# Attention stage: x given transposed and split on GpSimd, projections dealt out three halves to a graph

## The chip, the cores and the metric

The kernel runs on one core of a Trainium2 chip. A time is device microseconds (us) of one execution. TensorE (PE) does matmuls and transposes into PSUM; VectorE (DVE), ScalarE (ACT) and GpSimd (POOL) do the rest; SyncE (SP) issues most DMAs. Each engine works through its own instructions in order and waits on semaphores.

## What is computed

64 graphs of 128 nodes with 256 features, and a 128x128 adjacency for each. First an attention layer with eight heads, and a layernorm; the change touches only this. Then three layers of graph attention, each with a feed-forward part, and a last layernorm.

```
q = heads(x @ Wq); k = heads(x @ Wk); v = heads(x @ Wv)        # 8 heads of 32
scores = where(adj, q k^T / sqrt(32), -inf)                    # 128 x 128 per head
out = softmax(scores) @ v
x = layernorm(x + relu(out) @ Wo)
... three layers: scores = leaky(si + sj + b), softmax, agg, layernorm, gelu ffn, layernorm
```

## The kernel before

All work on attention is in the first `with ExitStack()` block, in steps t = 0 to 15 of four graphs each (j = 0 to 3; i = 4t + j). A step's tokens are 512 columns. The products with weights are made to higher precision from pairs: a number is split into a rounded part (`hi`) and a rest (`lo`), and `split_product` (its matmul is L45) sums three products for each half k of the 256 features. So a projection of 512 columns is two parts of three matmuls each, called halves in the text.

The order on each engine is written out by hand, and the engines are pipelined against each other over steps:

- TensorE, in step t and graph j: transposes of the softmax numerators of heads 4 to 7 (L383) and 0 to 3 (L389), of the reciprocal sums (L395), the products with v (L401, "PV"), the scores of graph i+2 (L365), the output product with Wo (L45 on `attT`). Between them `fill` puts work for coming steps: in graphs 0 to 2 two of the six projections of step t+1 (four q/k, two v), in graph 3 the eight transposes (`transpose_x`, L337) of x of step t+2 from `xq` into the PSUM banks `A`.
- ScalarE casts these banks to `xT_hi` (L439), copies the projections to SBUF (`proj_copy`, L444), takes the exponentials (L449), and copies transposes (L461, L469).
- VectorE subtracts for `xT_lo` (L511), adds the mask to the scores and takes maxima (`masked_scores`, L523: a graph's eight heads), and between or behind these the residual `y` (L573); it normalizes (L560), splits (L563, L565), and takes layernorm statistics (L535, L539).
- In graph 2 of step t, `masked_scores` is that of graph 0 of step t+1, and it needs the mask of step t+1, the first of the two that GpSimd makes.
- GpSimd (`body`, L313): `make_masks(t+1)` (L298 is the mask of this stage, L299 to L306 make another for the later stages), then `ln_group(t)`, the layernorm of step t, which waits for VectorE's statistics `mv_out`. These are made in graph 0 of step t+1. `hold_pool` waits and then runs a tiny instruction (`fence_pool`, L147).
- SyncE (`body`, L256), step t: load `xq` of t+2, store the second mask, wait for the last `y` of step t, load x and adjacency of t+2, wait for the layernorm of t, store it to `hist` (L270).

`mask1`, `hist` and `mask_hist` serve the later stages. `steps` runs t = 0 to 13 in a loop of two, and 14 and 15 behind it.

Of the kernel before, what the change touches and what calls it, by code (L numbers as in the profile page):

```python
# [24 lines left out]
F32 = mybir.dt.float32  # L25
# [5 lines left out]
P = 128  # L31
# [18 lines left out]
def gnn_kernel(nc, x_in, adj, Wq, Wk, Wv, Wo, attn_w, attn_b, W1, b1, W2, b2, g1, beta1, g2, beta2, out):  # L50
# [28 lines left out]
    with ExitStack() as whole:  # L79
# [91 lines left out]
        with ExitStack() as ctx:  # L171
# [4 lines left out]
            xq = sb("xq", [P, GROUP, D])  # L176
# [6 lines left out]
            xT = [sb("xT_hi", [P, KT, TOK], F32R), sb("xT_lo", [P, KT, TOK], F32R)]  # L183
# [17 lines left out]
            wa_split, xq_ld = sems("wa_split", "xq_ld")  # L201
            x_ld = sems("x_ld_even", "x_ld_odd")
            (masks_made, xT_made, xT_hi_out, xT_lo_out, proj_made, proj_out, s_made, scored, peaked, exped,
             pT_made, pT_out_b, pT_out_a, pv_made, den_inv, rden_out, rdenT_made, rdenT_out, att_out,
             attT_hi_out, attT_lo_out, wo_made, y_out, bn_out, eye_made, eye_added) = sems(
                "masks_made", "xT_made", "xT_hi_out", "xT_lo_out", "proj_made", "proj_out", "s_made", "scored",
# [32 lines left out]
            def _(e):  # L239
# [3 lines left out]

                for sem in stored + mask1_st:
                    e.sem_inc(sem, START)
                e.dma_start(xq[:], block_of(x_g, 0)).then_inc(xq_ld, 16)
# [4 lines left out]
                e.wait_ge(xT_made, 2)  # L251
                e.dma_start(xq[:], block_of(x_g, 1)).then_inc(xq_ld, 16)
# [31 lines left out]
            def _(e):  # L284
# [22 lines left out]

                make_masks(0, 0, 0)

# [17 lines left out]
            def _(e):  # L327
                e.wait_ge(ident_set, 1)

                def transpose_x(t1, k):  # L330

                    if k == 0:
                        e.wait_ge(xq_ld, 16 * (t1 + 1))
                    if not isinstance(t1, int) or t1:
                        e.wait_ge(proj_out, 6 * t1 - 1 + k)
                    for j in range(GROUP):
                        mm = e.transpose(A[k][:, j * N:(j + 1) * N], xq[:, j, k * P:(k + 1) * P], ident[:])  # L337
                    mm.then_inc(xT_made, 1)

                def project(t1, par, n, parts=(0, 1)):  # L340

                    bank = A[n % 2]
                    if n == 0 and 0 in parts:
                        e.wait_ge(xT_hi_out, 2 * (t1 + 1))
                        e.wait_ge(xT_lo_out, 2 * (t1 + 1))
                    if n >= 2 and 0 in parts:
                        e.wait_ge(proj_out, 6 * t1 + n - 1)
                    if n < 4:
                        mm = split_product(e, bank, (w_hi, w_lo), xT,
                                           lambda w, k: w[:, n % 2, k, (n // 2) * P:(n // 2 + 1) * P],  # L350
                                           lambda x, k: x[:, k, :], parts)
                    else:
                        for h in parts:
                            j = 2 * (n - 4) + h
                            mm = split_product(e, bank[:, h * D:(h + 1) * D], xT, (w_hi, w_lo),
# [13 lines left out]
                def fill(t, par, j, half, a1, a2, parts=(0, 1)):  # L369

                    if j < 3 and a1:
                        project(t + 1, 1 - par, 2 * j + half, parts)
                    if j == 3 and half == 0 and a2:
                        for k in parts:
                            transpose_x(t + 2, k)

                def body(q, par, a1, a2):
                    t = 2 * q + par
                    for j, i, _, (has2, t2, par2, j2) in graphs(q, par, a1):
# [5 lines left out]
                        fill(t, par, j, 0, a1, a2, parts=(0,))  # L385
# [5 lines left out]
                        fill(t, par, j, 0, a1, a2, parts=(1,))  # L391
# [17 lines left out]
                        fill(t, par, j, 1, a1, a2)  # L409
# [5 lines left out]
                for k in range(KT):  # L415
                    transpose_x(0, k)
# [4 lines left out]
                for k in range(KT):  # L421
                    transpose_x(1, k)
# [5 lines left out]
            def _(e):  # L428
# [7 lines left out]

                def xT_hi(t1, k):
# [759 lines left out]
```

## Time and profile before

| | us |
|---|---|
| median of 3 runs (1758.45 to 1760.78) | 1760.39 |
| the profiled execution | 1757.66 |
| its span | 1755.9 |
| TensorE busy in the span | 1631.8 (93%) |
| VectorE | 1372.9 (78%) |
| ScalarE | 1246.0 (71%) |
| GpSimd | 1232.0 (70%) |

The shares are means over the attention stage (to about 430 us) and the later stages. A share tells how much an engine works, not when it is free. So stretches of the attention stage and the order in which things stand on each engine are read beside it. In a timeline, what stands in brackets is how long the engine had been idle before, and which instruction of which engine ended it.

### The profile page before, as it was taken

What the parts mean: (1) busy time and instruction counts of PE and PEld (TensorE: products, weight loads), DVE (VectorE), ACT (ScalarE), POOL (GpSimd) and SP (SyncE); (2) the same over time, 40 slices, a digit from 0 to 9 for tenths busy, and PEclk for the clock granted to TensorE, in tenths of its full rate; (3) what the DMA queues carried; (4) which work ended last, traced back from release to release, by engine and by line L of the source; (5) the groups of instructions that cost most, each with busy time, mean ns of one, the idle gap of its engine ahead of it and who ended that gap; (6) DMA issues with size and microseconds to landing.
All of it is one profiled execution on the core that took longest, in us unless ns stands there. A gap on an engine that the chain in (4) does not pass through costs nothing.

```text
span 1755.9 us, 40514 instructions
## 1 busy us (share of the span) xinstructions
PE 1631.8 (93%) x12032; PEld 1441.2 (82%) x12032; DVE 1372.9 (78%) x5392; ACT 1246.0 (71%) x2884; POOL 1232.0 (70%) x2087
## 2 busy tenths in 40 slices
PE   4999999996599999999989999999999999999994
PEld 3877777774499899899979899899888888888894
DVE  2888888887678878787777877788787888888862
ACT  2888888885477767767757777767766777777763
POOL 3354445543368777777868778777868999999996
PEclk8999999998699999999999999999999999999997
DMA  6132223322212212212213122212211222222211
GB/s 195 50 96 83 78 78 96 96 77 74 81 40 96 96 36 72 72 37 70 72 36 96 61 70 72 72 36 72 72 36 61 70 74 72 73 94 72 73 49 48
DMA packets 152118, 127.41 MB, mean 73 GB/s; under 512 B 16512, under 2 KB 145024, under 8 KB 152064
## 3 DMA queue, kind: packets, MB, share of 16 engines
q1 hardware_dynamic: 145024, 124.30, 22.5%
q10 hardware_dynamic: 7040, 2.51, 0.6%
q8 instruction: 19, 0.31, 0.1%
q14 instruction: 35, 0.29, 0.1%
HBM read 89.04 MB, written 37.75 MB: 72 GB/s over the span
## 4 chain that ended last, share of the span: by engine, by line
PE 51%; POOL 16%; DVE 5%; issue 2%; ACT 1%; POOLq 0%; DVEq 0%; ACTq 0%
PE ps L45 22%; PE ps L879 22%; PE ps L852 3%; POOL xo L792 2%; POOL gnn_n L160 2%; POOL gnn_norm L786 2%; PE ps L866 2%; POOL gnn_norm L160 2%; POOL gnn_fin L805 2%; POOL inv L155 2%; DVE gnn_junk L1004 2%; PE ps L844 1%; POOL gnn_hb L775 1%; POOL gnn_hb L771 1%; PE ps L859 1%
## 5 line engine op out<-in xcount | busy, mean ns | idle before, releaser
L879 PE MATMUL ps<-gnn_w_hi,gnn_g_hi 128*128 128x256 f32 x1536 | 434.1, 283 | 0.0
L879 PE MATMUL ps<-gnn_w_lo,gnn_g_hi 128*128 128x256 f32 x1536 | 429.0, 279 | 0.0
L879 PE MATMUL ps<-gnn_w_hi,gnn_g_lo 128*128 128x256 f32 x1536 | 428.7, 279 | 0.0
L974 ACT ACTIVATE gnn_g_hi<-ps,b_cols 128x512 fp32r<-128x512 f32 x384 | 264.6, 689 | 206.9 <-PE ps L45 206.9
L45 PE MATMUL ps<-gnn_hT_hi,gnn_w_hi 128*128 128x512 f32 x768 | 339.5, 442 | 4.2 <-DVE gnn_g_lo L1075 4.2
L1075 DVE TENSOR_TENSOR gnn_g_lo<-ps,gnn_g_hi 128x512 fp32r<-128x512 f32 x384 | 262.7, 684 | 95.9 <-ACT ps L975 95.5
L45 PE MATMUL ps<-gnn_hT_hi,gnn_w_lo 128*128 128x512 f32 x768 | 304.0, 396 | 0.0
L45 PE MATMUL ps<-gnn_hT_lo,gnn_w_hi 128*128 128x512 f32 x768 | 303.8, 396 | 0.0
L879 PEld LDWEIGHTS ps<-gnn_w_lo,gnn_g_hi 128*128 128x128 f32 x1536 | 288.9, 188 | 2.2
L879 PEld LDWEIGHTS ps<-gnn_w_hi,gnn_g_hi 128*128 128x128 f32 x1536 | 288.8, 188 | 2.2
L879 PEld LDWEIGHTS ps<-gnn_w_hi,gnn_g_lo 128*128 128x128 f32 x1536 | 288.7, 188 | 0.0
L975 ACT ACTIVATE ps<-ps,b_cols 128x512 f32<-128x512 f32 x384 | 250.6, 653 | 0.0
L1004 DVE CUSTOM_DVE_ANT_0 gnn_junk<-x,aw 128x256 f32<-128x256 f32 x384 | 222.7, 633 | 0.5 <-PEq L171 0.5
L449 ACT ACTIVATE att_probs<-att_probs,att_neg_peak 128x128 f32<-128x128 f32 x512 | 199.1, 393 | 10.7 <-DVE att_neg_peak L530 10.7
L45 PEld LDWEIGHTS ps<-gnn_hT_hi,gnn_w_lo 128*128 128x128 f32 x768 | 144.8, 189 | 34.5
L45 PEld LDWEIGHTS ps<-gnn_hT_hi,gnn_w_hi 128*128 128x128 f32 x768 | 145.5, 189 | 32.9 <-DVE gnn_g_lo L1075 5.0
L45 PEld LDWEIGHTS ps<-gnn_hT_lo,gnn_w_hi 128*128 128x128 f32 x768 | 145.5, 190 | 28.0
L775 POOL TENSOR_TENSOR gnn_hb<-gnn_hb,affine 128x256 f32<-128x256 f32 x192 | 156.3, 846 | 7.2 <-POOL gnn_hb L771 6.0
L949 ACT ACTIVATE gnn_hT_hi<-ps,beta_cols,g_cols 128x512 fp32r<-128x512 f32 x96 | 74.9, 780 | 109.8 <-PE ps L866 109.8
L152 POOL TENSOR_TENSOR inv<-gnn_mv,eps 128x4 f32<-128x4 f32 x96 | 19.5, 203 | 186.8 <-DVE gnn_mv L1143 153.6
L1067 DVE TENSOR_TENSOR gnn_res<-ps,gnn_hb 128x256 f32<-128x256 f32 x192 | 79.9, 416 | 85.3 <-PE ps L879 84.7
L771 POOL TENSOR_TENSOR gnn_hb<-gnn_n,affine 128x256 f32<-128x256 f32 x192 | 138.9, 755 | 8.5 <-POOL gnn_n L160 7.2
(126 smaller groups left out, 3952.2 us busy)
## 6 DMA issues: line engine op xcount, KB each, us to landing
hist<-xo SPq DMA_DIRECT2D x48, 512.0 KB, 3.7
x<-hist SPq DMA_DIRECT2D x48, 512.0 KB, 3.8
aw<-in_L_gnn_attn_w SPq DMA_DIRECT2D x48, 256.0 KB, 4.1
gmask<-mask_hist SPq DMA_DIRECT2D x48, 256.0 KB, 4.0
att_xq<-in_x SPq DMA_DIRECT2D x16, 512.0 KB, 4.6
att_xl<-in_x SPq DMA_DIRECT2D x16, 512.0 KB, 3.7
gnn_fin<-hist SPq DMA_DIRECT2D x16, 512.0 KB, 3.9
out<-gnn_fin SPq DMA_DIRECT2D x16, 512.0 KB, 3.0
```

Source lines behind the costliest of these rows:

```text
L45: last = pe.matmul(out, w_of(w[a], k), x_of(x[b], k), start=(n == 0 and k == 0), stop=(n == len(terms) - 1 and k == 1))
L160: last = e.tensor_scalar(dest[:, j, :], y[:, j, 0:D], inv[:, 2, j:j + 1], inv[:, 3, j:j + 1], ALU.mult, ALU.add)
L449: ins = e.activation(probs[b][:, h, :], probs[b][:, h, :], ACT.Exp, bias=neg_peak[b][:, h:h + 1], scale=SCALE, accum_out=den[b][:, h:h + 1])
L771: ins = e.tensor_tensor(hb[par1][:, j, :], n1[:, j, :], row(l, 0), ALU.mult)
L775: ins = e.tensor_tensor(hb[par1][:, j, :], hb[par1][:, j, :], row(l, 2), ALU.add)
L879: mm = e.matmul(FF2[j % 2], g[a][:, m, j * N:(j + 1) * N], V[b][:, m, :], start=(n == 0), stop=(n == len(terms) - 1))
L949: e.activation(hT[0][:, k, :], HT[k], ACT.Identity, bias=shift, scale=gain)
L974: e.activation(g[0][:, m, :], FF1[FFB[m]], ACT.Gelu, bias=bias)
L975: e.activation(FF1[FFB[m]], FF1[FFB[m]], ACT.Gelu, bias=bias).then_inc(gelu_out, 1)
L1004: ins = e.tensor_tensor_reduce(out=junk[:, j, n, :], in0=x[par2][:, j, 0:D], in1=aw[par2][:, n, :], scale=1.0, scalar=0.0, op0=ALU.mult, o ...
L1067: e.tensor_tensor(y2[:, j, :], FF2[j % 2], hb[par][:, j, :], ALU.add).then_inc(y2_out, 1)
L1075: e.tensor_tensor(g[1][:, m, :], FF1[FFB[m]], g[0][:, m, :].bitcast(F32), ALU.subtract).then_inc(g_lo_out, 1)
```

## The change

The host gives x also as `xT`: per step 128 rows (features) of 1024 numbers (two halves of the features, 512 tokens each), 4 KB a row. SyncE loads it into `xT_raw` in place of `xq`. GpSimd makes `hi` and `lo` from it with `split_xT`, four casts and four subtractions of 128x256, at the start of its step t for step t+2. `xT` becomes two pairs of buffers, used by even and odd steps. TensorE's transposes, ScalarE's casts and VectorE's subtractions for it go. `fill` hands out the twelve halves as three to each of four graphs, beginning in graph 3 of the step before. ScalarE's `proj_copy` calls are spread in the same way. In `masked_scores` the residual stands after four heads in each graph, before that only in graph 3.

```diff
@@ sync @@
+                def load_xT(t):
+                    e.dma_start(xT_raw[:].rearrange("p k n -> p (k n)"),
+                                xT_in[bass.ds(t, 1)].rearrange("o p n -> p (o n)")).then_inc(xT_ld, 16)
...
-                e.wait_ge(xT_made, 2)
-                e.dma_start(xq[:], block_of(x_g, 1)).then_inc(xq_ld, 16)
+                e.wait_ge(xT_lo_out, 1)
+                load_xT(1)
...
                 def body(q, par, more):
                     t = 2 * q + par
                     if more:
-                        e.wait_ge(xT_made, 2 * (t + 2))
-                        e.dma_start(xq[:], block_of(x_g, t + 2)).then_inc(xq_ld, 16)
+                        e.wait_ge(xT_lo_out, t + 2)
+                        load_xT(t + 2)
@@ gpsimd @@
+                PARTS = [(k, slice(n * TOK // 2, (n + 1) * TOK // 2)) for k in range(KT) for n in range(2)]
+
+                def split_xT(t1, par):
+
+                    hold_pool(e, xT_ld, 16 * (t1 + 1))
+                    if not isinstance(t1, int) or t1 >= 2:
+                        hold_pool(e, proj_made, 6 * (t1 - 1))
+                    hi, lo = xT[par]
+                    for k, half in PARTS:
+                        ins = e.tensor_copy(hi[:, k, half], xT_raw[:, k, half])
+                    ins.then_inc(xT_hi_out, 1)
+                    e.wait_ge(xT_hi_out, t1 + 1)
+                    for k, half in PARTS:
+                        ins = e.tensor_tensor(lo[:, k, half], xT_raw[:, k, half], hi[:, k, half].bitcast(F32), ALU.subtract)
+                    ins.then_inc(xT_lo_out, 1)
+
+                split_xT(0, 0)
                 make_masks(0, 0, 0)
+                split_xT(1, 1)
...
                 def body(q, par, a1, a2):
                     t = 2 * q + par
+                    if a2:
+                        split_xT(t + 2, par)
                     if a1:
                         e.wait_ge(masks_made, 2 * (t + 1))
                         e.wait_ge(peaked, GROUP * t + 1)
@@ tensor @@
                     if n == 0 and 0 in parts:
-                        e.wait_ge(xT_hi_out, 2 * (t1 + 1))
-                        e.wait_ge(xT_lo_out, 2 * (t1 + 1))
-                    if n >= 2 and 0 in parts:
+                        e.wait_ge(xT_lo_out, t1 + 1)
+                    if 0 in parts and (n >= 2 or not isinstance(t1, int) or t1):
                         e.wait_ge(proj_out, 6 * t1 + n - 1)
...
-                def fill(t, par, j, half, a1, a2, parts=(0, 1)):
-
+                def fill(t, par, j, slot, a1, a2):
+
+                    n, part = divmod(3 * ((j + 1) % GROUP) + slot, 2)
                     if j < 3 and a1:
-                        project(t + 1, 1 - par, 2 * j + half, parts)
-                    if j == 3 and half == 0 and a2:
-                        for k in parts:
-                            transpose_x(t + 2, k)
+                        project(t + 1, 1 - par, n, (part,))
+                    if j == 3 and a2:
+                        project(t + 2, par, n, (part,))
@@ scalar @@
-                        if j > 0 and a1:
-                            proj_copy(t + 1, 1 - par, 2 * (j - 1))
-                            proj_copy(t + 1, 1 - par, 2 * (j - 1) + 1)
+                        if a1:
+                            proj_copy(t + 1, 1 - par, (0, 2, 3, 5)[j])
...
+                        if a1 and j in (0, 2):
+                            proj_copy(t + 1, 1 - par, 1 if j == 0 else 4)
...
-
-                for k in range(KT):
-                    xT_hi(0, k)
@@ vector @@
-                            masked_scores(i + 2, t2, par2, j2, residual, at=4 if j == GROUP - 1 else NH)
+                            masked_scores(i + 2, t2, par2, j2, residual, at=4)
```

GpSimd, from the end of one layernorm (`xo`) to the masks of the next step; `xT_ld` counts the landed loads of the transposed x.

```order
 L160 TENSOR_SCALAR xo<-y,inv 128x256 x4
 L168 REGISTER_ALU
-L316 REGISTER_ALU [waits ln_out]
-L317 ISA [waits masks_made]
+L145 ISA [waits ln_out]
+L147 TENSOR_TENSOR fence_pool<-half_neg 128x1 [waits xT_ld]
+L145 REGISTER_ALU
+L147 TENSOR_TENSOR fence_pool<-half_neg 128x1 [waits proj_made]
+L321 CAST att_xT_hi<-att_xT_raw 128x256 x4
+L325 TENSOR_TENSOR att_xT_lo<-att_xT_raw,att_xT_hi 128x256 [waits xT_hi_out]
+L325 TENSOR_TENSOR att_xT_lo<-att_xT_raw,att_xT_hi 128x256 x3
```

Between the layernorm and the masks there now stand a wait for the load and eight operations.

SyncE at the turn from one step to the next, of the changed kernel.

```order
L274 ISA [waits ln_out]
L274 DMA hist<-xo 128x4x256
L263 REGISTER_ALU
L245 ISA [waits xT_lo_out]
L245 DMA att_xT_raw<-in_xT 128x1024
L266 REGISTER_ALU
L267 ISA [waits masks_made]
L267 DMA mask_hist<-att_mask_1 128x4x128
```

The load has the place that the load of `xq` had, behind the store of the layernorm; what it waits for is GpSimd's split, no longer TensorE's transposes.

TensorE in graph 3, before:

```order
L383 MATMUL ps<-ident,att_probs 128x128 x3
L333 ISA
L335 ISA [waits xq_ld]
L337 MATMUL ps<-ident,att_xq 128x128 [waits proj_out]
L337 MATMUL ps<-ident,att_xq 128x128 x3
L386 REGISTER_ALU
L389 MATMUL ps<-ident,att_probs 128x128 [waits y_out,exped]
```

and now:

```order
L397 MATMUL ps<-ident,att_probs 128x128 x3
L359 REGISTER_ALU
L361 ISA [waits xT_lo_out]
L45 MATMUL ps<-att_xT_hi,att_w_hi 128x512 [waits proj_out]
L45 MATMUL ps<-att_xT_lo,att_w_hi 128x512
L45 MATMUL ps<-att_xT_hi,att_w_lo 128x512
L400 REGISTER_ALU
L403 MATMUL ps<-ident,att_probs 128x128 [waits y_out,exped]
```

Where four transposes waited for a load, the first half of the next-but-one step's projections waits for GpSimd's subtractions.

## Rows read from the trace of the kernel before

**Rows 1.** Windows of a stretch: start:end us, length, busy (instructions) per engine, clock, DMA, GB/s
```profile
202.00:229.00 27.00, 25.22 (x282) 20.74 (x284) 23.36 (x114) 22.72 (x93) 14.74 (x24) 1.00 0.28 78
```

**Rows 2.** Timeline of SyncE's DMA issues: start us, us, engine line operation out<-in
```profile
73.86 0.40 SPq L270 DMA_DIRECT2D hist<-xo  x1
74.52 0.38 SPq L260 DMA_DIRECT2D att_xq<-in_x  x1
...
196.55 0.40 SPq L270 DMA_DIRECT2D hist<-xo  x1
197.50 0.38 SPq L260 DMA_DIRECT2D att_xq<-in_x  x1
...
392.54 0.40 SPq L270 DMA_DIRECT2D hist<-xo  x1
```

**Rows 3.** Timeline of GpSimd over one step, the same columns
```profile
192.25 0.20 POOL L152 TENSOR_TENSOR inv<-mv,eps 128x4 f32<-128x4 f32 x1 [12.47 <-DVE mv L539]
...
194.19 2.19 POOL L160 TENSOR_SCALAR xo<-y,inv 128x256 f32<-128x256 f32 x4
...
197.31 2.10 POOL L298 TENSOR_SCALAR att_mask<-att_adjl 128x512 f32<-128x512 int32 x1
...
202.94 0.34 POOL L147 TENSOR_TENSOR fence_pool<-half_neg 128x1 f32<-128x1 f32 x2
```

**Rows 4.** Timeline of VectorE over the same step
```profile
191.82 0.28 DVE L539 BATCH_NORM_AGGREGATE mv<-att_a_stats 128x2 f32<-128x6 f32 x3
...
205.81 0.29 DVE L523 CUSTOM_DVE_ANT_0 att_probs<-ps,att_mask 128x128 f32<-128x128 f32 x1
...
209.33 1.28 DVE L511 TENSOR_TENSOR att_xT_lo<-ps,att_xT_hi 128x512 fp32r<-128x512 f32 x2
210.53 0.41 DVE L560 SCALAR_TENSOR_TENSOR att_att<-ps,att_rdenT 128x256 f32<-128x256 f32 x1
...
215.88 0.28 DVE L539 BATCH_NORM_AGGREGATE mv<-att_a_stats 128x2 f32<-128x6 f32 x3
```

**Rows 5.** Timeline of TensorE, two places in this stage and one of a later stage
```profile
195.50 0.39 PE L45 MATMUL ps<-att_xT_lo,att_w_hi 128*128 128x512 f32 x1
195.73 0.40 PE L45 MATMUL ps<-att_xT_hi,att_w_lo 128*128 128x512 f32 x1
...
209.47 0.65 PE L401 MATMUL ps<-att_probsT,att_v 128*32 128x128 f32 x16
...
893.72 0.73 PE L45 MATMUL ps<-gnn_hT_hi,gnn_w_hi 128*128 128x512 f32 x1 [3.51 <-DVE gnn_g_lo L1075]
```

**Rows 6.** Part 6 of the page: DMA issues, count, KB each, us to landing
```profile
att_xq<-in_x SPq DMA_DIRECT2D x16, 512.0 KB, 4.6
att_xl<-in_x SPq DMA_DIRECT2D x16, 512.0 KB, 3.7
...
out<-gnn_fin SPq DMA_DIRECT2D x16, 512.0 KB, 3.0
```

**Rows 7.** Groups of GpSimd's instructions by line and shape: count | busy us, mean ns
```profile
L775 POOL TENSOR_TENSOR gnn_hb<-gnn_hb,affine 128x256 f32<-128x256 f32 x192 | 156.3, 846 | 7.2 <-POOL gnn_hb L771 6.0
...
L786 POOL TENSOR_TENSOR gnn_norm<-gnn_norm,affine 128x256 f32<-128x256 f32 x192 | 135.7, 740 | 8.1 <-POOL gnn_norm L160 6.8
...
L160 POOL TENSOR_SCALAR xo<-y,inv 128x256 f32<-128x256 f32 x64 | 35.2, 563 | 0.0
...
L306 POOL TENSOR_SCALAR att_mask<-att_eye_sum 128x512 f32<-128x512 f32 x16 | 31.1, 1943 | 1.1
...
L285 POOL MEMSET ident<- 128x128 f32 x1 | 0.2, 205 | 0.3 <-POOLq L1184 0.3
```

**Rows 8.** Windows of a later stretch, columns as in rows 1
```profile
890.00:895.00 5.00, 1.49 (x4) 1.10 (x4) 4.32 (x8) 1.43 (x3) 3.12 (x4) 0.88 0.00 2
```

**Rows 9.** Timeline of ScalarE at the start
```profile
27.03 1.07 ACT L444 COPY att_qk<-ps 128x512 f32<-128x512 f32 x2 [19.12 <-issue]
```

More of the change, by code:

```diff
@@ L182, in gnn_kernel @@
             mask1 = [sb(f"mask1_{i}", [P, GROUP, N]) for i in range(2)]
-            xT = [sb("xT_hi", [P, KT, TOK], F32R), sb("xT_lo", [P, KT, TOK], F32R)]
+            xT = [[sb(f"xT_hi{i}", [P, KT, TOK], F32R), sb(f"xT_lo{i}", [P, KT, TOK], F32R)] for i in range(2)]
             qk = [sb(f"qk{i}", [P, 4, TOK]) for i in range(2)]
@@ L384, in body @@
                         mm.then_inc(pT_made, 1)
-                        fill(t, par, j, 0, a1, a2, parts=(0,))
+                        fill(t, par, j, 0, a1, a2)
                         e.wait_ge(exped, 2 * i + 2)
@@ L390, in body @@
                         mm.then_inc(pT_made, 1)
-                        fill(t, par, j, 0, a1, a2, parts=(1,))
+                        fill(t, par, j, 1, a1, a2)
                         e.wait_ge(pT_out_b, i + 1)
@@ L408, in body @@
                             scores(i + 2, par2, j2)
-                        fill(t, par, j, 1, a1, a2)
+                        fill(t, par, j, 2, a1, a2)
                         e.wait_ge(attT_hi_out, i + 1)
@@ L420, in _ @@
                 scores(0, 0, 0)
-                for k in range(KT):
-                    transpose_x(1, k)
+                for slot in range(3):
+                    fill(-1, 1, 3, slot, True, True)
                 e.wait_ge(scored, 1)
@@ L455, in body @@
                     for j, i, has1, _ in graphs(q, par, a1):
-                        if j > 0 and a1:
-                            proj_copy(t + 1, 1 - par, 2 * (j - 1))
-                            proj_copy(t + 1, 1 - par, 2 * (j - 1) + 1)
+                        if a1:
+                            proj_copy(t + 1, 1 - par, (0, 2, 3, 5)[j])
                         e.wait_ge(pT_made, 2 * i + 1)
                         e.copy(probsT[:, 4:8, :].rearrange("p h n -> p (h n)"), PB[1]).then_inc(pT_out_b, 1)
-                        if j == 3 and a2:
-                            for k in range(KT):
-                                xT_hi(t + 2, k)
                         if has1 and j < 3:
@@ L488, in _ @@
                     proj_copy(0, 0, n)
-                for k in range(KT):
-                    xT_hi(1, k)
                 e.wait_ge(peaked, 1)
@@ L506, in split_weights @@
                     e.tensor_tensor(w_lo[:, pair], w_raw[:, pair], w_hi[:, pair].bitcast(F32), ALU.subtract).then_inc(wa_split, 1)
-                def xT_lo(t1):
-                    for k in range(KT):
-                        e.wait_ge(xT_hi_out, 2 * t1 + k + 1)
-                        e.tensor_tensor(xT[1][:, k, :], A[k], xT[0][:, k, :].bitcast(F32), ALU.subtract).then_inc(xT_lo_out, 1)
                 def masked_scores(i, t_, par, j, between=None, at=NH):
@@ L1188 @@
     arrays, args = {}, []
+    x = np.asarray(inputs["x"])
+    B, N, D = x.shape
+    laid = dict(inputs)
+    laid["xT"] = (x.reshape(B // GROUP, GROUP, N, D // P, P).transpose(0, 4, 3, 1, 2)
+                  .reshape(B // GROUP, P, D // P * GROUP * N))
+    names.insert(1, "xT")
     for name in names:
-        a = np.ascontiguousarray(inputs[name])
+        a = np.ascontiguousarray(laid[name])
         arrays[f"in_{name}"] = a
```

34 lines of the change are left out of this document (9 added, 25 removed).

## The prediction

> **What bounds the kernel now.** I read the span by stages first. The change touches the attention stage alone, sixteen steps of four graphs that fill the span to about 430 us; the rest stays as it is. In the stage's middle the stretches show TensorE busy 25.2 of 27 us, VectorE 23.4, ScalarE 22.7, and GpSimd 14.7 [rows 1]: two engines are nearly full, a third close behind, and GpSimd looks half idle. That share invites the change, and it is the number not to trust, since it says nothing of when GpSimd is free. So next I read SyncE's DMA issues and the order on GpSimd. SyncE stores step 0's result at 73.86 and step 13's at 392.54 [rows 2]: 318.68 us for 13 steps, 24.51 us a step. On GpSimd [rows 3] one step is: the layernorm of the step before (from 192.25, last piece ends at 194.19 + 2.19 = 196.38), then the masks of the step after, the first of which VectorE needs (197.31 to 199.41), then three more operations and a long wait. On VectorE [rows 4] the statistics that release the layernorm end at 191.82 + 0.28 = 192.10 (call this point V), and the first use of the new mask comes at 205.81 (call it M); the next V is at 215.88 + 0.28 = 216.16. So today the mask is ready 6.4 us before its use, and GpSimd sets nothing.
>
> **The change, part by part.** *What it takes away.* Per step, 8 transposes on TensorE, 2 casts on ScalarE and 2 subtractions on VectorE; the VectorE pair takes 1.28 us in the fourth graph [rows 4]. The fill of TensorE is evened out: now 4 halves in each of three graphs, then 3 in each of four. A half is three matmuls that start 0.23 us apart [rows 5], 0.70 us. In the first three graphs TensorE is what limits: 24.51 / 4 = 6.13 us a graph, less 0.70, is 5.43, and VectorE loses its 1.28 us in the fourth. If nothing else came late, a step would take about 22 us (4 x 5.43 = 21.7, and something for waits). Doing the residual after four heads instead of eight costs nothing; it only shortens the wait of the next transposes.
>
> *What it adds, and where.* GpSimd's step now begins with the split of x for step t+2, ahead of the masks of t+1. Its input is loaded by SyncE, in order, directly behind the store of the layernorm that GpSimd has just finished. So the load cannot start while GpSimd is busy elsewhere: it starts when GpSimd becomes free for it. In the kernel before the load stood at the same place, but its user was TensorE in the fourth graph, ten us later; now its user is the very next instruction on GpSimd. Behind that waiting instruction are queued the split, the masks of t+1, and the next layernorm. Who waits for them: TensorE (first half of step t+2's projections, in the fourth graph) and, later and harder, VectorE (the mask, at the end of the third graph).
>
> From V to M, each term:
> - layernorm: 192.10 to 196.38, 4.28 us [rows 3, 4].
> - store issued 0.17 after it, the load behind it 0.95 later, in other steps 0.66 [rows 2]: 0.81. Together 0.98.
> - landing. The load that it replaces, of equal size and with the same neighbours, takes 4.6 us; another load of 512 KB takes 3.7, the quickest transfer of 512 KB 3.0 [rows 6]. The new one is one run of 4 KB per partition. I take 4.2, between the first two, and keep 3.0 to 4.7.
> - two fences on GpSimd, 0.34 and a gap: 0.40 [rows 3].
> - four casts of 128x256. No cast stands on GpSimd here. The nearest row, a two-step scalar operation of the same size, takes 0.563; half of the 128x512 comparison is 0.97; a memset of 128x128 takes 0.205, so that 0.31 for 256 columns is a floor [rows 7]. I take the nearest: 2.25, and keep 1.2 to 3.9.
> - a wait between, 0.10, and four subtractions of 128x256 with two inputs: 0.740 to 0.846 [rows 7], taken 0.80: 3.20.
> - from there to the first mask 0.50 (today 0.93 with the layernorm's own wait in it), the mask 2.0, VectorE's start 0.1 [rows 3].
>
> Sum: 4.28 + 0.98 + 4.20 + 0.40 + 2.25 + 0.10 + 3.20 + 0.50 + 2.0 + 0.1 = 18.0 us.
>
> The row of the two-step operation gives 2.2 ns per column. The Trainium skill, GPSIMD Engine Reference, section 4.1 Engine selection, says instead that with one input GpSimd runs at roughly line rate, which would make a cast about 0.3 us by my estimate from that page; the sum would fall by 1.0 us, 13 us over the stage, and the sign would stay. No run so far shows which.
>
> From M to the next V the order of work is VectorE's, and today's rows give it: 216.16 - 205.81 = 10.35 us [rows 4]. The two subtractions go from it (1.28 us from 209.33), but the product that they stood before has to wait for TensorE anyway: the PV matmuls run from 209.47 to 210.12, so it moves from 210.53 to 210.2 at best [rows 4, 5]. That leaves 10.0. The cycle V, M, V closes on itself, once a step: 18.0 + 10.0 = 28.0 us. At the free pace VectorE would be ready for the mask 22 - 10.0 = 12 us after V and so stands about 6 us; by then everything else is late by the same.
>
> *The clock.* In the loop TensorE will have gaps of about 2 us (until the split is done) and 3 us (until the mask is). After a gap of 3.51 us in a later stage [rows 5] the granted clock of the stretch falls to 0.88 of full, that is to 1.2 GHz of 2.4 for part of it [rows 8]. At half speed PV and the transposes after M could come some 0.5 us later. I put in 0.3, range 0 to 1: 28.3 us a step.
>
> Steps 1 to 13 each have a split in front of the next mask: 13 x (28.3 - 24.51) = +49 us. Step 14 splits nothing and runs at the free pace, -2; step 0 has its mask long before and runs at the free pace, -2; step 15 has the earlier residual, -1. At the start ScalarE issues its small loads only after the two casts, from about 7.9, and does its first copy at 27.03 after 19.12 us of issuing [rows 9]; without the casts it may begin up to 6 us earlier, and TensorE's projections wait for it. The DMA engines are full then, so I take 4, range -1 to 6, and 1 for the second split that leaves VectorE. The first split on GpSimd ends at about 11, as late as VectorE's today. Together -10.
>
> **Sum** against the profiled execution: 1757.7 + 49 - 10 = 1797. That execution lies 2.7 below the median of 1760.4, so the median becomes **1799 us**, 2.2% slower.
>
> **The rivals.**
> *A. Faster: GpSimd is hidden.* Then all fifteen steps with a successor run at the free 22 us: 15 x -2.5 = -38, and -5 at the start: 1717. For it: GpSimd's share, and that it idles after the masks. Against it: that idle time is after its late work, not before. It decides if V to M is under 12 us, so that load, casts and subtractions together are under 3.6, less than the shortest landing and two casts.
> *B. No change.* The +49 must shrink to the 10 us of gains: a step of 25.3 us, V to M 15.3, load and split together 6.9 instead of 9.6. The floors of the three add up to 3.0 + 1.2 + 3.0 = 7.2. Time 1757 to 1764. This rival is the lower bound of all unknown terms at once.
> *C. Slower still.* Landing 4.7, casts at 0.97 (3.9) and subtractions at 0.85 (3.4) make V to M 20.4, and with 0.7 us of clock a step 31.1 us: 13 x 6.6 - 10 = +76, 1836. For it: the split runs beside VectorE's copies in SBUF, and the comparison row is slow without a reason that I can see.
> *D. The change doesn't do what it says.* If SyncE's load were ahead of the store, the landing would hide and it would be A. The order of its queue excludes that: it waits for the layernorm, stores, and only then loads.
> The Trainium skill, DMA: Bandwidth & Descriptors, gives a fixed 2.0 us and 436 GB/s for a transfer; by that the load lands in 3.2 us (my estimate from that page), the step is 1.0 us shorter and the median 1786; still the forecast's side.
>
> **How the numbers follow.** Forecast (a step of 26.3 to 30, V to M of 16 to 20) 0.74; C 0.16; B 0.05; A 0.05. The range begins with landing and casts both four fifths of the way to their floors (3.2 and 1.4, a step of 26.4 with 0.2 of clock: 13 x 1.9 - 10 = +15, 1775) and ends with C: 1773 to 1836. What a measurement of this kernel can tell from no change is about 0.2%, 3.5 us. Chances: faster by more 0.06, within 0.03, slower by more 0.91.
>
> **What would show it.** In the changed kernel: steps of about 28 us between SyncE's stores; GpSimd idle about 5 us after each layernorm, released by the DMA of the transposed x; VectorE idle 5 to 6 us before the first head of the third graph's scores, released by GpSimd's mask; TensorE idle about as long in the fourth graph, first on GpSimd's split, then on VectorE's residual. The first doubt is the casts' duration, the second the landing. The prediction is wrong in kind if VectorE does not wait for the mask, or if steps of 22 us appear before step 14.

## The result, and the profile after

| | before | after |
|---|---|---|
| median of 4 runs, us | 1760.57 | 1811.70 (1808.87 to 1812.87) |
| span of the profiled execution | 1755.9 | 1810.1 |
| us a step, stores of step 0 to 13 | 24.51 | 28.40 |
| TensorE busy in the span | 1631.8 (93%) | 1649.3 (91%) |

The changed kernel is slower, by a ratio of 1.0291 (95% interval 1.0273 to 1.0309). 1799 had been predicted, with 1773 to 1836 as the range. SyncE's DMA issues answer to [rows 2]; the columns here, and in the timelines below, are start us, us, engine, line, operation, out<-in, and in brackets the idle time before and what ended it:

```profile
74.53 0.40 SPq L274 DMA_DIRECT2D hist<-xo  x1
...
215.82 0.40 SPq L274 DMA_DIRECT2D hist<-xo  x1
216.75 0.35 SPq L245 DMA_DIRECT2D att_xT_raw<-in_xT  x1
...
443.68 0.40 SPq L274 DMA_DIRECT2D hist<-xo  x1
...
468.00 0.39 SPq L274 DMA_DIRECT2D hist<-xo  x1
```

(443.68 - 74.53) / 13 = 28.40 us. So 369.15 - 318.68 = 50.5 us of the span's +54.2 lie in steps 1 to 13. The rest is small: the first store comes 0.7 later than in before, step 14 takes 24.32 (in before its store is at 416.52, a step of 23.98), and what follows it takes 1342.1, before 1339.4.

One step on GpSimd after, to be laid beside [rows 3]:

```profile
213.49 2.17 POOL L160 TENSOR_SCALAR xo<-y,inv 128x256 f32<-128x256 f32 x4
221.28 0.34 POOL L147 TENSOR_TENSOR fence_pool<-half_neg 128x1 f32<-128x1 f32 x2 [5.62 <-DMA att_xT_raw<-in_xT]
221.56 1.49 POOL L321 CAST att_xT_hi<-att_xT_raw 128x256 fp32r<-128x256 f32 x4
223.13 3.02 POOL L325 TENSOR_TENSOR att_xT_lo<-att_xT_raw,att_xT_hi 128x256 fp32r<-128x256 f32 x4
...
226.38 1.95 POOL L302 TENSOR_SCALAR att_mask<-att_adjl 128x512 f32<-128x512 int32 x1
```

The layernorm ends at 215.66, SyncE stores at 215.82 and loads at 216.75, and GpSimd stands idle until the load has landed. Only then come the casts, the subtractions and, at 226.38, the mask that began 0.93 us behind the layernorm in before.

The same step on VectorE, beside [rows 4]:

```profile
211.12 0.28 DVE L535 BATCH_NORM_AGGREGATE mv<-att_a_stats 128x2 f32<-128x6 f32 x3
...
224.00 0.70 DVE L557 CAST att_attT_hi<-att_att 128x256 fp32r<-128x256 f32 x1
224.73 0.83 DVE L559 TENSOR_TENSOR att_attT_lo<-att_att,att_attT_hi 128x256 fp32r<-128x256 f32 x1
228.48 0.06 DVE L142 MEMSET fence_dve<- 128x1 f32 x1 [2.91 <-POOL att_mask L302]
228.52 0.29 DVE L519 CUSTOM_DVE_ANT_0 att_probs<-ps,att_mask 128x128 f32<-128x128 f32 x1
...
237.73 0.42 DVE L567 TENSOR_TENSOR y<-ps,att_xl 128x256 f32<-128x256 f32 x1 [1.86 <-PE ps L45]
...
240.96 0.28 DVE L535 BATCH_NORM_AGGREGATE mv<-att_a_stats 128x2 f32<-128x6 f32 x3
```

V is at 211.40, M at 228.52, the next V at 241.24: 17.1 and 12.7 us. In the step behind it M comes at 258.12 and V at 269.19: 16.9 and 11.1. VectorE is idle 2.91 us in front of the mask.

The waits of the stretch 80 to 440 us; the columns are who waits, for whom, us in total, times, longest:

```profile
POOL inv L152 <- DVE mv L535: 77.5, 13, 7.5
POOL fence_pool L147 <- DMA att_xT_raw<-in_xT: 71.0, 13, 5.6
...
DVE fence_dve L142 <- POOL att_mask L302: 32.9, 12, 2.9
...
PE ps L403 <- DVE y L567: 25.0, 13, 2.2
```

The chain is in these lines: GpSimd waits for the load, VectorE for GpSimd, TensorE for VectorE's residual, once in every step. In its windows (columns as in [rows 1]):

```profile
202.00:229.00 27.00, 23.12 (x240) 17.43 (x238) 19.70 (x103) 18.94 (x78) 15.22 (x29) 1.00 0.27 78
229.00:256.00 27.00, 23.71 (x227) 18.59 (x228) 20.55 (x106) 18.41 (x77) 13.81 (x29) 0.87 0.25 78
```

VectorE is busy 19.7 us of 27 instead of 23.4, and ScalarE 18.9 instead of 22.7: no engine is full any longer. In the second window the granted clock is 0.87 of full, so for a part of it TensorE has 1.2 GHz instead of 2.4, and the step took 29.9 us. Three of the thirteen steps are like that (step lengths of 29.90, 29.85 and 29.86 between stores), the other ten take 27.95 on average. Two of these ten have the lower clock too, for a smaller part of the step:

```profile
273.61:302.15 28.54, 24.47 (x242) 18.78 (x240) 20.40 (x108) 18.65 (x78) 16.32 (x29) 0.94 0.26 73
330.14:358.05 27.91, 24.58 (x242) 18.44 (x240) 20.41 (x110) 19.00 (x80) 16.35 (x29) 0.94 0.25 75
```

The eight steps at full clock take 27.89 on average.

### The profile page after: what moved, and what is told of

It is laid out like the page before. It is cut to its first block, busy times and chain, and to the rows that moved or that the text cites. A ratio compares the mean times of both kernels' runs of the same rounds, so it can differ in the third digit from the quotient of the medians.

```text
span 1810.1 us, 40318 instructions
## 1 busy us (share of the span) xinstructions
PE 1649.3 (91%) x11904; PEld 1433.1 (79%) x11904; DVE 1357.8 (75%) x5360; ACT 1224.4 (68%) x2852; POOL 1303.6 (72%) x2245
## 4 chain that ended last, share of the span: by engine, by line
PE 49%; POOL 16%; DVE 5%; issue 2%; ACT 1%; POOLq 0%; DVEq 0%; ACTq 0%
PE ps L45 21%; PE ps L871 21%; PE ps L844 3%; POOL xo L784 2%; POOL gnn_n L160 2%; POOL gnn_norm L778 2%; PE ps L858 2%; POOL gnn_norm L160 2%; POOL gnn_fin L797 2%; DVE gnn_junk L996 2%; POOL inv L155 2%; PE ps L836 1%; POOL gnn_hb L767 1%; POOL gnn_hb L763 1%; PE ps L851 1%
## 5 line engine op out<-in xcount | busy, mean ns | idle before, releaser
L457 ACT ACTIVATE att_probs<-att_probs,att_neg_peak 128x128 f32<-128x128 f32 x512 | 199.2, 392 | 25.5 <-DVE att_neg_peak L526 25.3
```

The lines of the kernel that those rows point to most:

```text
L457: ins = e.activation(probs[b][:, h, :], probs[b][:, h, :], ACT.Exp, bias=neg_peak[b][:, h:h + 1], scale=SCALE, accum_out=den[b][:, h:h + 1])
```

## The experiments

Each is compared with the kernel before, run on the same chip; its median was 1755.5 to 1757.8 there, against 1760.6 beside the changed kernel. So kernels measured on different chips are compared by their ratios, and steps by their traces. My theory was the cycle V, M, V with the load in it. The rivals were that the order on GpSimd alone (split ahead of mask) does it, that the early residual or the dealing of the halves does, or that the clock does.

### Masks first, whole

```diff
-                    if a2:
-                        split_xT(t + 2, par)
                     if a1:
                         e.wait_ge(masks_made, 2 * (t + 1))
                         e.wait_ge(peaked, GROUP * t + 1)
                         make_masks(q + (par + 1) // 2, 1 - par, t + 1)
+                    if a2:
+                        split_xT(t + 2, par)
```

> The changed kernel with GpSimd's step in another order: both masks of step t+1 first, then the split of step t+2. Theory T (the mask comes late because the load of the transposed x and the split stand in front of it): VectorE's waits for the mask go. But the split then ends about 17.9 us after VectorE's statistics, and TensorE wants it at about 15.5 (the first half in the fourth graph), so a wait of 2 to 3 us moves to TensorE: a step of about 27 us for 28.4, 1793 us, 1785 to 1800. Rival R (not GpSimd but TensorE's new distribution sets the pace, three halves in the fourth graph in front of the next statistics): no change, 1811.

Measured: 1795.28 us, 1.0223 (ratio to the kernel before; 1.0205 to 1.0241), 27.36 us a step, as expected. One wait of 80 to 440 us, and the end of GpSimd's step:

```profile
PE ps L45 <- POOL att_xT_lo L325: 23.9, 13, 3.0
```

```profile
217.78 1.93 POOL L310 TENSOR_SCALAR att_mask<-att_eye_sum 128x512 f32<-128x512 f32 x1
219.80 0.34 POOL L147 TENSOR_TENSOR fence_pool<-half_neg 128x1 f32<-128x1 f32 x2
220.08 1.69 POOL L321 CAST att_xT_hi<-att_xT_raw 128x256 fp32r<-128x256 f32 x4
221.84 2.79 POOL L325 TENSOR_TENSOR att_xT_lo<-att_xT_raw,att_xT_hi 128x256 fp32r<-128x256 f32 x4
```

The wait for the mask is gone, and so is GpSimd's wait for the load, which lands beside the masks. In their place TensorE waits for the split, up to 3.0 us, in the fourth graph. This order is worth only 1.0 us a step; GpSimd's work stays in the cycle, by its other exit.

### First mask, split, then the second mask

```diff
                                     ALU.is_equal, ALU.mult).then_inc(masks_made, 1)
+                    if between:
+                        between()
...
-                    if a2:
-                        split_xT(t + 2, par)
...
-                        make_masks(q + (par + 1) // 2, 1 - par, t + 1)
+                        make_masks(q + (par + 1) // 2, 1 - par, t + 1,
+                                   (lambda: split_xT(t + 2, par)) if a2 else None)
```

> The changed kernel with the split between the first mask, which VectorE needs, and the three operations for the second mask, which only a store waits for. T: the mask is there 7 us after the statistics (wanted at 14), the split at about 15 (wanted by TensorE at 15.5), neither waits: a step of 24.3 to 24.8 us, 1763 us, 1755 to 1770. The load's landing is hidden behind the mask for 2 us only, so a small wait on TensorE may stay. R: no change, 1811.

Measured: 1770.85, 1.0088 (1.0071 to 1.0104), 25.26 us a step. No engine waits for the mask or the split. GpSimd still waits for the load, but less, and nobody waits for that:

```profile
POOL fence_pool L147 <- DMA att_xT_raw<-in_xT: 34.9, 13, 3.0
```

This order, with nothing else changed, gives back 3.1 of the 3.9 us that a step had lost. The time is just above my range, since the pace without waits is not what I took it for (below).

### The load a step earlier, into a second buffer

```diff
-            xT_raw = sb("xT_raw", [P, KT, TOK])
+            xT_raw = [sb(f"xT_raw{i}", [P, KT, TOK]) for i in range(2)]
...
                         e.wait_ge(xT_lo_out, t + 2)
-                        load_xT(t + 2)
+                        load_xT(t + 3, 1 - par)
```

The split stays ahead of the masks. The input has one step more at its end, so that the last load has something to read.

> The changed kernel with a second buffer for the transposed x, loaded one step earlier; the split stays in front of the masks. It tells the load's landing from the split's own time. T: the 5.6 us that GpSimd stands for the load in each step go, the mask comes about 11.5 us after the statistics (wanted at 14), no engine waits for GpSimd: a step of 24.3 to 24.8 us, 1763 us, 1755 to 1772. If the split alone were enough to make the mask late, a wait for the mask would stay and the time would be 1780 or more. R: no change, 1811.

Measured: 1771.69, 1.0092 (1.0075 to 1.0108), 25.40 us a step, with no wait for the load and none for the mask. This isolates the load. 3.0 us a step, 39 us of the stage, hang on when this one DMA starts (by the ratios 1.0291 and 1.0092, 35 us). The split at its place ahead of the mask costs little once its input is there: the next experiment, with the split out of the way, is 0.4 us a step better.

### The split in GpSimd's idle time

```diff
-                        e.wait_ge(xT_lo_out, t + 2)
-                        load_xT(t + 2)
+                        e.wait_ge(xT_lo_out, t + 3)
+                        load_xT(t + 3)
...
-                    if a2:
-                        split_xT(t + 2, par)
                     if a1:
...
                         make_masks(q + (par + 1) // 2, 1 - par, t + 1)
+                    if a2:
+                        split_xT(t + 3, 1 - par)
```

The load is a step earlier as well (one buffer is enough), and step 2 is split ahead of the loop.

> The changed kernel with the split moved into GpSimd's idle time: in step t the masks of t+1, then the split of t+3, then the layernorm of t; the load is issued one step earlier into the one buffer. T: as the kernel with the early load, 1763 us, 1753 to 1770; the free pace of the new order is then seen undisturbed. If it is at 22 us a step, as the prediction had it, 1735; I now expect 24.3 or more, since in the changed kernel's undisturbed graphs the distance from one normalization to the next is 6.0 to 6.1 us although TensorE has a half less. R: no change, 1811.

Measured: 1763.12, 1.0042 (1.0025 to 1.0059), 25.04 us a step. Here nothing waits for GpSimd. So 25.0 is the free pace of the changed kernel's other parts. It is above the 24.51 of before, where I had put 22, though TensorE, ScalarE and VectorE all have less to do.

### The residual late again, in both settings

```diff
-                            masked_scores(i + 2, t2, par2, j2, residual, at=4)
+                            masked_scores(i + 2, t2, par2, j2, residual, at=4 if j == GROUP - 1 else NH)
```

First on top of the last experiment, then on the changed kernel itself.

> The kernel with the split in GpSimd's idle time, and the residual again behind all eight heads in the first three graphs. In its trace VectorE waits 0.27 us for the output product in front of each early residual, and a graph is one ring: copy of the transposes, PV, normalization, two splits, output product, residual, four more heads, and what stands behind. Theory L (the ring bounds a graph, not TensorE's amount of work): with eight heads in the output product's shadow the ring is shorter by those 0.27 us, three graphs a step, 0.8 us a step, 15 steps: 1751 us, 1747 to 1758. Rival W (the amount of work on TensorE or VectorE bounds it): no change, 1763.

> The changed kernel with nothing but the residual put back behind eight heads in the first three graphs. Under T the cycle over the mask sets the step; of it only the first graph's order lies behind the mask's arrival, and the residual of the fourth graph is early in both. So nothing or little: 1808 to 1813 us. If the early residual were what made the changed kernel slow (the rival), it would fall by 12 us or more, under 1800.

Measured, with the split in idle time: 1743.69, 0.9937 (0.9920 to 0.9953), 23.84 us a step, 18 us better by the ratios than without this line, and better than the 1747 to 1758 that I had expected. On the changed kernel itself: 1816.82, 1.0346 (1.0329 to 1.0363), 29.18 us a step; against the changed kernel's 1.0291 that is 0.5% or some 10 us worse. So the early residual costs 1.2 us a step where the pace is free, and it is not what makes the changed kernel slow. There TensorE's wait for the residual, which has become late, grows, from 25.0 us in 80 to 440 us to

```profile
PE ps L403 <- DVE y L567: 45.8, 13, 3.5
```

and the clock falls in twelve of the thirteen steps, in the changed kernel in five. The one step at full clock takes 28.24 us, about as much as the longest such step of the changed kernel (27.55 to 28.18), so most of the loss goes with the lower clock:

```profile
189.02:217.26 28.24, 23.32 (x242) 17.66 (x240) 20.80 (x111) 19.39 (x81) 16.37 (x29) 1.00 0.26 74
```

I had expected 1808 to 1813 and missed that.

### The early residual alone, on the kernel before

```diff
-                            masked_scores(i + 2, t2, par2, j2, residual, at=4 if j == GROUP - 1 else NH)
+                            masked_scores(i + 2, t2, par2, j2, residual, at=4)
```

> The kernel before with only the residual moved up behind four heads in all graphs. There TensorE has four halves in these graphs and the output product ends only 0.04 us before the residual starts, so the early residual waits for it, and VectorE idles instead of doing four heads first. TensorE's order isn't changed, and it bounds these graphs. Under L and W alike: no gain, a loss of 0 to 0.3 us in three graphs a step, 1756 to 1770 us against 1756.

Measured: 1790.44, 1.0200 (1.0182 to 1.0219), 26.67 us a step. I had expected 1756 to 1770, and this is the largest miss of the study. A timeline row of VectorE, and its waits in 100 to 380 us:

```profile
204.42 0.42 DVE L573 TENSOR_TENSOR y<-ps,att_xl 128x256 f32<-128x256 f32 x1 [0.78 <-PE ps L45]
```

```profile
DVE y L573 <- PE ps L45: 28.3, 42, 1.0
```

VectorE has done four heads and waits for the product with Wo, with four heads still to do. Heads 4 to 7 of the scores, and with them ScalarE's exponentials and TensorE's next transposes, are behind this wait. Done last, the residual finds the product ready. So it is no free edit: it puts TensorE and VectorE in series, once a graph. A part of the 35 us is the clock, which falls in eight of the thirteen steps, and in none of them in before. Here is a step with it and one without:

```profile
232.98:260.31 27.33, 24.60 (x250) 20.30 (x249) 21.09 (x113) 20.66 (x80) 11.61 (x19) 0.94 0.26 77
260.31:286.13 25.82, 23.21 (x250) 18.93 (x250) 21.19 (x113) 20.44 (x81) 11.75 (x19) 1.00 0.27 81
```

The five steps at full clock take 25.86 us on average, against 24.51 in before, and the eight others 27.18. So of the 2.2 us a step the early residual's waits cost 1.35 and the clock that falls with them 0.8.

### TensorE kept busy

```diff
+                    for _ in range(warm):
+                        e.matmul(bank, w_hi[:, 0, 0, 0:P], x_pair[0][:, 0, :], start=True, stop=True)
...
-                        project(t + 2, par, n, (part,))
+                        project(t + 2, par, n, (part,), warm=6 if slot == 0 else 0)
```

Six matmuls whose results are overwritten, ahead of the fourth graph's first half, on the changed kernel.

> The changed kernel with six matmuls of 128x512 more in front of the fourth graph's first half, each a group of its own whose result is overwritten; they take 1.4 us and lie in the gap of 2.2 us in which TensorE waits for VectorE's residual. It asks what the fallen clock costs: in the changed kernel steps with a granted clock of half for 6.8 us take 29.9 us instead of 27.9. If the gap makes the clock fall, it stays at full now and 5 to 8 us are won: 1804 to 1807 us. If the clock falls for another reason, no change, or a loss of up to 1.4 us a step if the gap isn't there when they run (1811 to 1829).

Measured: 1806.32, 1.0289 (1.0272 to 1.0307), 27.81 us a step. The windows of the same two stretches:

```profile
202.00:229.00 27.00, 24.18 (x243) 18.20 (x241) 19.68 (x103) 18.95 (x78) 15.49 (x28) 1.00 0.26 78
229.00:256.00 27.00, 24.07 (x244) 18.64 (x245) 20.01 (x102) 18.97 (x78) 15.38 (x30) 1.00 0.26 78
```

The granted clock stays full, and a step costs 0.6 us less than in the changed kernel's trace, 8 us in thirteen steps, of which the start gives 2 back. The median lies in my range of 1804 to 1807, but by the ratios, 1.0289 and 1.0291, no gain can be told at all. So the clock follows the waits here and costs 0 to 8 of the 51 us; it isn't their cause.

### Statistics in a gap of VectorE

```diff
+                        if j > 0:
+                            statistics(i - 1, par, j - 1)
...
-                        if j < GROUP - 1:
-                            statistics(i, par, j)
```

A graph's statistics stand behind the next graph's copy of the transposes (L548), where VectorE waits for PV. Once on top of the split in idle time with the late residual, once on the kernel before.

> The kernel with the split in GpSimd's idle time and the late residual, and in addition the layernorm statistics of graphs 0 to 2 taken one graph later, behind the copy of the transposes, where VectorE idles 0.84 us for PV in each graph; today they stand in front of that copy. L (a graph is a ring of VectorE's and TensorE's work in series): 0.34 us leave the ring in three graphs a step, 1.0 us a step, 13 to 15 us: 1730 us, 1726 to 1738, unless TensorE's own work (5.33 us a graph) ends the gain sooner. W (VectorE's amount of work bounds it): no change, 1744, as its work is the same.

> The kernel before with the same move of the statistics. There TensorE's four halves in graphs 0 to 2 make the second transposes late (they end at 202.60, the copy starts at 202.64), so VectorE's work in front of the copy lies in their shadow. L: little, 0 to 5 us: 1751 to 1756 us. If the move were worth 13 us here too, it would have nothing to do with the dealing out of the halves.

Measured: 1737.23, 0.9889 (0.9873 to 0.9906), 23.46 us a step, and on the kernel before 1758.55, 1.0014 (1.0004 to 1.0023), where I had expected 1751 to 1756. VectorE's wait for PV in 100 to 380 us, first without this edit, then with it:

```profile
DVE att_att L557 <- PE ps L418: 30.7, 36, 0.9
```

```profile
DVE att_att L559 <- PE ps L418: 15.2, 29, 0.6
```

Half of the wait is filled, and the step is 0.4 us shorter, where I had expected 1.0. On the kernel before the same edit gains nothing: in three steps the clock falls and they take 25.5 to 25.8 us, and the other ten take 24.49 on average, as the 24.51 of before. So its pace hangs on something else (as I read it, on the four halves in a graph; not shown). In the fastest version TensorE is nearly full:

```profile
180.00:300.00 120.00, 117.24 (x1240) 90.85 (x1241) 106.43 (x561) 97.33 (x403) 82.96 (x150) 1.00 0.31 93
```

It is busy 117.2 of 120 us. This version beats both kernels, the one before by 1.1%.

### Four halves in each of three graphs again

```diff
-                    n, part = divmod(3 * ((j + 1) % GROUP) + slot, 2)
-                    if j < 3 and a1:
-                        project(t + 1, 1 - par, n, (part,))
-                    if j == 3 and a2:
-                        project(t + 2, par, n, (part,))
+                    if j < 3 and a1:
+                        project(t + 1, 1 - par, 2 * j + slot // 2, ((0,), (1,), (0, 1))[slot])
```

With `proj_copy` moved back to match: once on the fastest version, once on the changed kernel.

> The kernel with the split in idle time, late residual and moved statistics, and the twelve halves handed out as before the change: four to each of graphs 0 to 2, none to graph 3, ScalarE's copies accordingly. It tells what dealing out three to a graph is worth when nothing else is in the way. L: graphs 0 to 2 take TensorE's 6.0 us, graph 3 about 5.1: 23.2 us a step against 22.9: 1735 to 1745 us. If the distribution doesn't matter, as the version with three.

> The changed kernel with the halves handed out as before the change (four to each of graphs 0 to 2, none to graph 3), all else as changed. Measured in the changed kernel: from the mask's arrival to the next statistics 11.1 us in a step at full clock, where the prediction had 10.0. Theory: the 1.1 us are TensorE's three halves, which now stand in graph 3 and in front of the products that the statistics wait for. Then it falls by up to 13 x 1.1 = 14 us, to 1797 us, if the clock doesn't fall more often; TensorE's gap in graph 3 gets longer, so it may, and then up to 10 us come back: 1797 to 1812. Rival (the halves in graph 3 cost nothing, and the prediction only misread VectorE's own work): 1810 us or more, and graph 3 as long at full clock as in the changed kernel.

Measured: 1753.28, 0.9980 (0.9971 to 0.9990), 24.34 us a step, 16 us slower than the same kernel with three halves to a graph, and above the 1735 to 1745 that I had expected. On the changed kernel: 1827.17, 1.0401 (1.0382 to 1.0420), 29.21 us a step. I had thought that halves away from graph 3 would shorten M to V there, and expected 1797 to 1812: wrong. The granted clock of its windows:

```profile
202.00:229.00 27.00, 22.70 (x221) 18.05 (x221) 17.92 (x96) 17.78 (x73) 14.22 (x23) 0.87 0.25 75
229.00:256.00 27.00, 22.29 (x233) 18.04 (x232) 19.65 (x102) 18.41 (x78) 16.42 (x29) 0.94 0.20 60
```

Without halves to fill the fourth graph the clock falls in both stretches, and in all thirteen steps. In steps where it is as low as in the three long ones of the changed kernel, M to V is 12.4 us in most, against 12.7 to 12.9 there. So at the low clock the halves in the fourth graph do cost some 0.4 us; that the clock now falls in every step outweighs it. What they cost at full clock this run doesn't tell.

## Why the prediction was right

**The cycle**, its direction and its size were right: 28.40 us a step against 28.3. By the ratios, the load a step earlier takes 35 us off and the split out of the cycle 44. The rivals A, B and D are out, and C's slow casts did not come. (The lower end of the range comes to 1775 by its own sum, where 1773 is written; nothing hangs on it.) The agreement in the sum is better than that of its terms, though, since several errors cancel.

**V to M: 18.0 put, 16.9 and 17.1 in the two steps shown.** The largest error is the casts. Groups of GpSimd in 60 to 430 us (count, then busy us and mean ns of one), beside [rows 7]:

```profile
L325 POOL TENSOR_TENSOR att_xT_lo<-att_xT_raw,att_xT_hi 128x256 fp32r<-128x256 f32 x52 | 38.7, 775 | 1.0
...
L321 POOL CAST att_xT_hi<-att_xT_raw 128x256 fp32r<-128x256 f32 x52 | 19.5, 415 | 0.0
```

Four casts take 1.49 us where I put 2.25: the nearest row was a two-step operation, and the floor of 1.2 was nearer. The subtractions are 0.775 each, 3.02 for four, against 3.20. The Trainium skill, GPSIMD Engine Reference, section 4.1 Engine selection, gives roughly line rate for one input, about 0.3 us by my estimate from it; this trace agrees better with that than with my row, with 0.415 us alone and 0.37 in a run of four. The landing went the other way, by the page's list of DMA issues, beside [rows 6]:

```profile
att_xT_raw<-in_xT SPq DMA_DIRECT2D x16, 512.0 KB, 4.5
```

4.5 us against the 4.2 taken and 4.6 of the load it replaces; runs of 4 KB instead of 1 KB changed little. The Trainium skill, DMA: Bandwidth & Descriptors, section Anatomy of one DMA — SWDGE (gpsimd) path, has 2.0 us and 436 GB/s, so 3.2 by my estimate; it fits them to DMAs that GpSimd issues, and this one is SyncE's. This trace, with 4.5 us, doesn't agree, and the row of the neighbour was the better guide.

**M to V: 10.0 put, 11.1 in five of the eight steps at full clock, 10.9 in the mean of the eight.** I took VectorE's list of work from before and let it run on. The rows show where most of the 1.1 us comes from. First a step of the changed kernel at full clock, with M at 258.12 and V at 269.19, then a row of the kernel before, in the step with M at 230.19 and V at 241.11:

```profile
260.97 0.49 DVE L545 COPY att_rden_cols<-att_rden 128x256 f32<-128x256 f32 x1
...
262.89 0.42 DVE L554 SCALAR_TENSOR_TENSOR att_att<-ps,att_rdenT 128x256 f32<-128x256 f32 x1 [0.83 <-PE ps L415]
263.35 0.52 DVE L557 CAST att_attT_hi<-att_att 128x256 fp32r<-128x256 f32 x1
...
267.31 0.20 DVE L543 RECIPROCAL att_rden<-att_den 128x8 f32<-128x8 f32 x1 [0.38 <-issue]
```

```profile
239.23 0.20 DVE L547 RECIPROCAL att_rden<-att_den 128x8 f32<-128x8 f32 x1 [0.38 <-issue]
```

- My 10.35 came from a short step. In the kernel before M to V alternates, 10.4 in one step and 10.9 in the next, with few exceptions, and 0.38 of the difference is this idle time of VectorE. In the changed kernel five of the eight steps at full clock have it; the other three take 10.6 to 10.9.
- The 0.35 that I took off for the subtractions did not come. The normalization (L554) begins 4.77 us behind M, in before 4.72. PV starts only when VectorE's copies in front of it are done, and they end 0.33 later, 0.20 of it in the first, which takes 0.49 us instead of 0.29 beside GpSimd's work.
- The cast takes 0.52 instead of 0.29, beside GpSimd's second mask (L310, 261.79 to 263.72).

Two other causes, the early residual and the three halves of graph 3, don't show in these rows. With the residual late again on the changed kernel, its one step at full clock still has 11.06 us from M to V. And TensorE, behind a half of graph 3, waits 0.73 us for VectorE's copy there (the matmul at 261.60).

**The clock: 0.3 put, about 0.5 measured.** The eight steps at full clock take 27.89, all thirteen 28.40: 0.51; with TensorE kept busy a step is 0.59 shorter. TensorE at half rate, in the second of the three long steps, beside [rows 5]:

```profile
229.94 0.63 PE L403 MATMUL ps<-ident,att_probs 128*128 128x128 f32 x4 [2.16 <-DVE y L567]
...
232.59 1.08 PE L415 MATMUL ps<-att_probsT,att_v 128*32 128x128 f32 x16
```

PV takes 1.08 us instead of 0.65, behind a gap of 2.16. Every step has a gap there (25.0 us in 13 waits), and eight of the thirteen keep their clock.

**The free pace: 22 us put, 25.0 measured.** This is the step that failed: "TensorE is what limits", so three matmuls less are 0.70 us less a graph. Two things were wrong in it. I took 0.70 us from the mean graph of 6.13 four times over, but the twelve halves are all still there: three graphs lose one, and the fourth gains three. On TensorE a step loses only eight transposes. Four of them take 0.43 us in before (208.53 to the next matmul at 208.96), so 24.51 less 0.9, 23.6 us, is the estimate that I should have made. The fastest version points the same way: TensorE is busy 117.24 of 120 us at 23.46 us a step, 22.9 us, more than the 22 that I had for the whole step. (Busy time isn't work alone: the kernel before has 111.19 of 120, 22.7 a step, with the transposes in it.) And the residual after four heads, which "costs nothing", costs 1.2 us a step where nothing waits for GpSimd, and 1.35 on the kernel before, besides what the clock takes there. Without it the pace is 23.8. It didn't hurt the sum in steps 1 to 13, where the cycle decides. It did hurt two of my smaller reasons: VectorE reaches the mask about 14 us after V, not 12, and idles 2 to 3 us there, not 5 to 6. And TensorE never waits for the split in the changed kernel; it comes to that half later than the split does.

**The ten us of gains** did not come. Step 14 takes 24.32, not 22; what follows it costs 2.7 more; the start gains nothing. Behind step 14 it is step 15 that is longer, 25.78 us to its store where before has 22.06, and the granted clock is lower in it (first the changed kernel, then before); what it would take at the same clock no run tells:

```profile
468.00:494.00 26.00, 14.34 (x108) 10.61 (x108) 15.29 (x73) 10.48 (x39) 4.93 (x11) 0.55 0.10 31
```

```profile
417.00:439.00 22.00, 10.41 (x108) 7.36 (x107) 14.22 (x71) 9.45 (x35) 4.94 (x11) 0.79 0.11 37
```

ScalarE at the start, beside [rows 9]:

```profile
14.55 6.13 ACTq L488 DMA_DIRECT2D g_cols<-in_L_gnn_g  x1
...
26.81 1.28 ACT L452 ACT_TABLE_LOAD   x1 [26.81 <-issue]
28.10 1.08 ACT L452 COPY att_qk<-ps 128x512 f32<-128x512 f32 x2
```

It begins to issue its small loads at 1.80 instead of 7.33, but a single issue now takes up to 6.13 us, and it is through at 26.77 against 26.99. The activation table, which before was loaded at 1.80 ahead of the casts, now comes behind the loads. I had called the gain uncertain because the DMA engines are full, and still taken 4 us of it. So +39 was forecast and +54.2 came in the span: of the 15.2 missed, 1.5 are in the steps and 13.7 in these small terms.

## What to carry to other kernels

A half-idle engine can take work only if the input is there when the engine is free and somebody's deadline isn't behind it: look at what starts the input's load and what is queued behind the wait, and load a step ahead. What taking work from a full engine gives is the work that leaves it over a whole step, not what leaves the fullest part; measure that pace with everything new out of the way before putting it in a sum. An edit that looks like a mere detail of order, such as a residual after four heads instead of eight, deserves its own run.

## What the runs showed of the hardware

- Beside GpSimd's subtractions, VectorE's cast of 128x256 takes 0.70 us instead of 0.29 to 0.30, and its subtraction 0.83 instead of 0.43 (224.00 and 224.73 in the changed kernel; the short ones at 211.95 and 212.28). Both engines work in SBUF. It isn't special to the split: in the kernel before the cast takes 0.69 at 155.71, beside GpSimd's second mask. In both kernels, from 60 to 430 us, every such cast (L563, in the changed kernel L557) with GpSimd idle takes 0.29 to 0.30. I had feared the opposite, a slower GpSimd: its subtractions take 0.775 us there.
- A DMA issue on ScalarE takes 0.44 us at 0.81 and 6.13 us at 14.55. From 14 to 27 us the DMA engines are full (busy share 1.08 in the windows view); that this is the reason I didn't test. Issuing earlier only meant waiting in the issue here.
- TensorE has a gap of about 2 us in each step (25.0 us in 13 waits), and the clock falls in five of the thirteen, in three of them for longer. With six matmuls of 128x512 in front of the fourth graph's first half it stays at full in all thirteen.
